# Batch 0's first attention with both token halves side by side in PSUM, strip-wise score passes for the last batch, and new instruction orders on five queues

## What is computed

```python
x = layernorm(x + attn(x))        # A: ternary-weight linear layers; softmax over the 16 heads of a token,
                                  #    plus a recurrent state over chunks of 128 tokens
x = layernorm(x + xattn(x, ctx))  # B: 32 query heads, 8 key heads, window 64, two sources (ctx and x)
x = layernorm(x + ffn(x))         # C: base linear layer + LoRA experts, top 2 of 8
```

## Time and profile before

| | us |
|---|---|
| median of 3 runs | 920.82 (917.58 to 921.01) |
| the profiled execution | 920.37 |
| its span, first to last instruction | 918.2 |
| PE busy | 805.0 (88%) |
| DVE busy | 515.8 (56%) |
| ACT busy | 322.8 (35%) |

### The profile page before, as it was taken

One profiled execution on the slowest core, in us unless ns is written; L12 is line 12 of the kernel. 1 busy time (PEld: TensorE's weight loads), 2 busy tenths in 40 slices (PEclk: granted clock), 3 DMA queues, 4 the chain that ended last, 5 costly groups with the idle time before them and its releaser, 6 DMA issues.

```text
span 918.2 us, 22670 instructions
## 1 busy us (share of the span) xinstructions
PE 805.0 (88%) x10223; PEld 518.4 (56%) x10275; DVE 515.8 (56%) x1061; ACT 322.8 (35%) x423; POOL 85.5 (9%) x103
## 2 busy tenths in 40 slices
PE   3888977888999989988899989988898978998996
PEld 2464763467635874467635864567545864474343
DVE  4645386437945487437845486447845383425233
ACT  5252323442243323442244323432244314230422
POOL 1102002000210012000300012000300010010001
PEclk9999999999999999999999999999999999999999
DMA  9512501000001000010001000010001000000000
GB/s 343 181 47 46 72 1 24 25 2 1 11 15 47 2 2 24 1 48 1 25 1 47 2 2 24 1 47 2 1 1 47 3 1 1 24 2 1 1 24 24
DMA packets 18879, 27.08 MB, mean 29 GB/s; under 512 B 5464, under 2 KB 7640, under 8 KB 18784
## 3 DMA queue, kind: packets, MB, share of 16 engines
q1 hardware_dynamic: 18640, 25.61, 9.3%
q10 hardware_dynamic: 144, 0.03, 0.0%
HBM read 21.44 MB, written 4.19 MB: 28 GB/s over the span
## 4 chain that ended last, share of the span: by engine, by line
PE 62%; DVE 19%; ACT 13%; issue 4%; POOL 1%; DMA 1%; ACTq 0%; POOLq 0%; SPq 0%; DVEq 0%
ACT p_b L740 9%; DVE max_b L1457 7%; PE ps L1118 7%; PE ps L1154 6%; PE ps L1039 6%; PE ps L1195 5%; PE ps L1022 4%; PE ps L1083 4%; PE ps L1059 3%; PE ps L870 2%; PE ps L943 2%; PE ps L1127 2%; PE ps L953 2%; PE ps L1047 2%; PE ps L838 2%
## 5 line engine op out<-in xcount | busy, mean ns | idle before, releaser
L740 ACT ACTIVATE p_b<-ps 128x2048 f32<-128x2048 f32 x64 | 106.5, 1664 | 116.1 <-PE ps L1127 116.1
L1457 DVE TENSOR_REDUCE max_b<-ps 128x4 f32<-128x768 f32 (+2 forms) x160 | 106.5, 709 | 39.5 <-PE ps L1097 21.3
L1083 PE MATMUL ps<-k_b,q_b 32*128 32x192 f32 (+2 forms) x1024 | 55.7, 332 | 25.7 <-DVE max_b L1457 23.6
L1118 PE MATMUL ps<-q_b,k_b 32*128 32x512 f32 (+1 forms) x512 | 66.2, 586 | 12.8 <-ACT p_b L740 7.0
L1483 DVE STREAM_TRANSPOSE o_nat<-ps 128x512 f32<-128x512 f32 x32 | 21.0, 695 | 98.2 <-PE ps L1143 98.2
L1083 PEld LDWEIGHTS ps<-k_b,q_b 32*128 32x128 f32 x1024 | 39.2, 184 | 43.1 <-DVE max_b L1457 37.1
L1143 PE MATMUL ps<-p_b,v_b 128*32 128x256 f32 (+1 forms) x1024 | 61.7, 358 | 2.0 <-ACT p_b L740 2.0
L1022 PE MATMUL ps<-c_t,wq 128*128 128x256 f32 x256 | 60.4, 385 | 2.9 <-DVE out_a L1380 1.9
L1337 DVE SCALAR_TENSOR_TENSOR nat<-ps,st_a,qkv_bias 128x512 f32<-128x512 f32 x48 | 35.3, 738 | 48.0 <-PE ps L870 47.7
L1195 PE MATMUL ps<-base_t,x_t 128*128 128x512 f32 x128 | 62.0, 609 | 0.3 <-DVE x L1562 0.3
L1039 PE MATMUL ps<-x_t,wq 128*128 128x256 f32 x256 | 60.0, 384 | 0.2 <-ACT x_t L694 0.2
(11 more groups left out here) (193 smaller groups left out, 1414.2 us busy)
## 6 DMA issues: line engine op xcount, KB each, us to landing
x_in<-x SPq DMA_DIRECT2D x8, 512.0 KB, 3.6
p_b<-ctx SPq DMA_DIRECT2D x8, 512.0 KB, 4.3
y<-x SPq DMA_DIRECT2D x7, 512.0 KB, 3.0
p_b<-L_attn_qkv_w SPq DMA_DIRECT2D x2, 1024.0 KB, 6.6
p_b<-L_xattn_Wq SPq DMA_DIRECT2D x1, 2048.0 KB, 14.8
x<-L_attn_qkv_w SPq DMA_DIRECT2D x2, 512.0 KB, 9.6
x<-L_ffn_base_w SPq DMA_DIRECT2D x2, 512.0 KB, 7.8
wo<-L_xattn_Wo SPq DMA_DIRECT2D x8, 128.0 KB, 7.5
```

What stands on the lines that cost most here:

```text
L740: act.activation(p_b[:, j % 2, :, 0:cols], ps[:, 4:8, 0:cols], ACT.Exp, scale=DB ** -0.5).then_inc(pb_here.sem, 1)
L1083: pe.matmul(bank(4 + r)[:, (i % 2) * N:(i % 2) * N + 2 * n * S], q_b[strip[r], i, :, :].rearrange("p h q -> p (h q)"), k_b[strip[r], half, ...
L1118: pe.matmul(bank(4 + r)[:, 0:nb * P], k_b[strip[r], half, 2 * j:2 * j + 2, :, :].rearrange("p c s k -> p (c s k)"), q_b[strip[r], 2 * j:2 ...
L1457: ins = dve.tensor_reduce(max_b[:, half, 0, i:i + k, 2 * n:2 * n + 2], ps[:, 4 + 2 * n:6 + 2 * n, :].rearrange("p r (i n) -> p i r n", i=2 ...
```

## The change

1. For batch 0 alone, half 1 of A uses banks 4 to 7 (`a_bank`), its own `maxp_0`, `maxt_0` and a `p_0` that lies over `q_b` and `k_b` (made one tile, `qk_b`). The order is `a2_s 0, a2_s 1, a2_m 0, a2_x 0, a2_m 1, a2_x 1, a2_v 0, a2_v 1` on PE; `a2_max 0, a2_max 1, a2_out 0, a2_out 1` on DVE; `b1_mix, a2_m 0, a2_m 1, a2_x 0, a2_x 1` on ACT. One more small load fills `maxp_0`.
2. `keep_on` goes out of `a2_m` (11), `a2_v` (6) and, for t = 1, `a2_s` (8).
3. The copy of the projection signs moves from DVE to ACT (`proj_keep`), between `a1_q` and `a1_v`; the two sums of absolute values move ahead, between two transposes of half 1. `proj_total` and `proj_scale` move behind `a2_rec`.
4. `base_turn 0` moves behind batch 1's `a1`, `base_turn 1` behind batch 1's six `a1_qkv`; ACT copies them ahead of batch 0's `a4`.
5. SP issues `mix` right after `late`, ahead of batch 0's context.
6. For batch 7, `b2` runs in two passes, strips 0 and 1 and then 2 and 3, and each waits only for the reduction of its own two banks; its `keep_on` goes out.
7. The lists of PE, DVE, ACT, POOL and SP are new. On PE the loop begins elsewhere in the same cycle, and inside it `b1_k` and `b1_q 0` go ahead of `a2_v 0`, `b1_v` behind it, `b2(0, 0)` ahead of `a2_x 1`, `a2_v 1` directly ahead of `a2_rec`; of C, `c2(1, 1)` goes ahead of `b3_s 3`. For batch 7, the parts of batch 6's `c2` are placed elsewhere among `b2` and `b3`.

```diff
+        def apart(b, t):
+            return isinstance(b, int) and b == 0 and t == 1
+        def a_bank(b, t):
+            return 4 if apart(b, t) else 0
...
             def a2_s(b, t, quarters):
-                    keep_on(b, 0, 8 if t else 4)
+                    keep_on(b, 0, 0 if t else 4)
...
+                        elif apart(b, t):
+                            pe.wait_ge(kept.sem, 3)
+                            pe.wait_ge(pkept.sem, 1)
                         else:
                             outa_here(pe, b, 1)
...
             def a2_m(b, t):
-                    keep_on(b, 0, 11)
...
             def a2_v(b, t):
-                    keep_on(b, 0, 6)
                     pa_here(pe, b, t + 1)
+                    src = p_0 if apart(b, t) else p_a
...
             def a2_x(b, t):
-                if t == 1:
+                if t == 1 and not apart(b, t):
                     oa_full(act, b, 1)
...
             def base_turn(b, part):
...
+                    out1(pe, 0)
+                    ct_here(pe, 0)
...
             def b2(b, half, pair):
-                keep_on(b, NB - 1, (0, 0, 6, 6, 4, 4, 2, 2)[4 * half + pair])
...
+                for strips in ((range(2), range(2, 4)) if alone else (range(4),)):
+                    if alone and pair:
+                        sb_max(pe, b, 8 * half + 2 * pair - 1 + strips[0] // 2)
...
```

The loop's order on PE around the second half of A, before and after:

```diff
-(B, of(b1_q, 1, range(2))), (A, of(a2_m, 1)), (B, of(b1_q, 1, range(2, KT))), (A, of(b1_c, 0)), (A, of(b1_c, 1)),
-(A, of(a2_x, 1, range(HT))), (B, of(b2, 0, 0)), (B, of(b2, 0, 1)), (A, of(a2_v, 1)), (B, of(b2, 0, 2)), (A, a2_rec),
+(B, of(b1_q, 1, range(2))), (A, of(b1_c, 0)), (B, of(b1_q, 1, range(2, KT))), (A, of(b1_c, 1)), (A, of(a2_m, 1)),
+(B, of(b2, 0, 0)), (A, of(a2_x, 1, range(HT))), (B, of(b2, 0, 1)), (A, of(a2_v, 1)), (A, a2_rec), (B, of(b2, 0, 2)),
```

More of the change, by code:

```diff
@@ L215, in program @@
         maxt_a = sb("maxt_a", [P, P], BF16)
+        maxp_0 = sb("maxp_0", [P, HT, S], BF16)
+        piece_0 = [maxp_0[:, :, p:3 * HT:3] for p in range(3)]
+        maxt_0 = sb("maxt_0", [P, P], BF16)
         sum_a = sb("sum_a", [P, HA, DA])
@@ L511, in c2 @@
                 sp.dma_start(one(ov, b), z_c[:, :, :]).then_inc(y_sent.sem, 16)
-            first = [(0, late), (0, b1), (1, a0), (2, a0), (1, mix)]
-            last = [(6, b1), (7, b1), (4, c2), (5, c2), (6, c2), (7, c2)]
-            run(sp, first, [(B, b1), (NEXT, a0), (D_, c2)], last)
+            first = [(0, late), (1, mix), (0, b1), (1, a0), (2, a0), (1, b1)]
+            last = [(7, b1), (4, c2), (5, c2), (6, c2), (7, c2)]
+            run(sp, first, [(D_, c2), (A, b1), (NEXT, a0)], last)
             y_sent(sp, NB - 1, 32)
@@ L916, in a2_s @@
                             rows = slice(a * S, (a + 1) * S)
-                            pe.matmul(bank(a), tokhot[rows, :], other[rows, :], start=True, stop=False)
+                            pe.matmul(bank(a_bank(b, t) + a), tokhot[rows, :], other[rows, :], start=True, stop=False)
                     for c in quarters:
@@ L1066, in b2 @@
             def b2(b, half, pair):
[L1067 to L1077 removed]
+                alone = isinstance(b, int) and b == NB - 1
@@ L1078, in b2 @@
+                if pair == 0:
+                    if half:
+                        mb_here(pe, b, 1)
+                    else:
+                        q_here(pe, b)
+                        k_here(pe, b)
+                        v_here(pe, b)
+                        if not alone:
+                            ct_here(pe, b + 1)
+                elif not alone:
+                    sb_max(pe, b, 8 * half + 2 * pair)
                 seen = [(i, slice(max(i - 2, 0), i + 1)) for i in (2 * pair, 2 * pair + 1)]
@@ L1079, in b2 @@
                 o = lambda r, i, n: bank(4 + r)[:, (i % 2) * N:(i % 2) * N + 2 * n * S].rearrange("p (c k) -> p c k", c=n)
-                for i, keys in seen:
-                    n = min(i, 2) + 1
-                    for r in range(4):
-                        pe.matmul(bank(4 + r)[:, (i % 2) * N:(i % 2) * N + 2 * n * S], q_b[strip[r], i, :, :].rearrange("p h q -> p (h q)"),
-                                  k_b[strip[r], half, keys, :, :].rearrange("p c s k -> p (c s k)"),
-                                  start=(i % 2 == 0), stop=False, skip_group_check=True)
@@ L1204, in _ @@
             first = [(-1, early), (0, a1), (0, of(a1_qkv, 0, [0])), (0, of(a1_qkv, 0, [1])), (0, of(a1_qkv, 0, [2])), (0, of(a1_qkv, 1, [0])),
-                     (0, of(a1_qkv, 1, [1])), (0, of(a1_qkv, 1, [2])), (0, a1_qt), (0, a1_state), (0, late), (0, of(a1_v, 0)), (0, of(a1_v, 1)),
-                     (0, of(a2_s, 0, range(HT))), (0, of(a2_m, 0)), (0, of(a2_x, 0, range(HT))), (0, proj_total), (0, of(a2_v, 0)),
-                     (0, of(a2_s, 1, range(HT))), (0, of(base_turn, 0)), (0, of(a2_m, 1)), (0, of(a2_x, 1, range(HT))), (0, of(base_turn, 1)),
@@ new lines, in _ @@
+                     (0, of(a1_qkv, 1, [1])), (0, of(a1_qkv, 1, [2])), (0, a1_state), (0, a1_qt), (0, late), (0, of(a1_v, 0)), (0, of(a1_v, 1)),
+                     (0, of(a2_s, 0, range(HT))), (0, of(a2_s, 1, range(HT))), (0, of(a2_m, 0)), (0, of(a2_x, 0, range(HT))), (0, of(a2_m, 1)),
+                     (0, of(a2_x, 1, range(HT))), (0, of(a2_v, 0)), (0, of(a2_v, 1)), (0, of(b1_c, 0)), (0, of(b1_c, 1)), (0, a2_rec), (0, proj_total),
+                     (0, of(b1_qc, 0, range(2))), (0, of(b1_qc, 0, range(2, KT))), (0, b1_kc), (0, a3_t), (0, of(a3, 0)), (0, of(a3, 1)), (1, a1),
@@ new lines, in _ @@
+                     (0, of(base_turn, 0)), (1, of(a1_qkv, 0, [0])), (1, of(a1_qkv, 0, [1])), (1, of(a1_qkv, 0, [2])), (1, of(a1_qkv, 1, [0])),
+                     (1, of(a1_qkv, 1, [1])), (1, of(a1_qkv, 1, [2])), (0, of(base_turn, 1)), (0, of(b1_qc, 1, range(2))), (1, a1_qt),
+                     (0, of(b1_qc, 1, range(2, KT))), (0, of(b1_x1, 0)), (0, of(b1_x1, 1)), (1, a1_state), (1, of(a1_v, 0)), (0, of(b1_v, range(2))),
+                     (1, of(a1_v, 1)), (0, of(b1_q, 1, range(2))), (1, of(a2_s, 0, range(HT))), (0, of(b1_q, 0, range(2))),
@@ L1354, in a2_max @@
                             dve.wait_ge(w_in.sem, W_IN)
+                    at = a_bank(b, t)
+                    part = piece_0 if apart(b, t) else piece
                     for n in range(2):
```

350 lines of the change are left out of this document (176 added, 174 removed).

## The result

The changed kernel takes 913.40 us (median of 14 runs, 911.25 to 916.12), the kernel before 918.51 on the same chip (14 runs, 915.84 to 921.21). The ratio is 0.9939, with a 95% interval of 0.9923 to 0.9955. That is faster by 5.1 us, against a forecast of 13.3. The profiled executions differ more, 920.37 against 913.30 us (spans 918.2 and 911.2). The profiled one of before lies in the upper part of its runs, so the traces show a gain of 7.0 where the medians show 5.1. The granted clock says why in part. The profiled one had 0.995. So what follows is read against an execution of before with more low clock than most of its executions have.

A forecast was written before the change was run, and what follows sets the result against it. It took PE as busiest (88%), with both ends bound by latency. Head -8.0, loop 0 and tail -5.3 summed to -13.3 us: 907.1 from the profiled 920.37, forecast 907, range 900 to 914.5.

The forecast's parts named there:

- the ladder: Batch 0's A block: with its two halves overlapped, the recurrent part is complete 10.8 us earlier, before the clock's cost.
- the 1.1 us that I took for `a2_x`: Batch 0's A block: one clock drop to 1.2 GHz, on `a2_x`, makes it 1.1 us late.
- the base weight: `base_turn` moved to batch 1's projections, with the reordered list there: +1.4 us up to batch 1's scores.
- the second part of the turn: `base_turn 1`, behind batch 1's `a1_qkv`: stands in full on the path, +1.1 us; the reordered list adds 0.8.
- The head: Start of the kernel up to the loop: -9.4 to the projection and +1.4 for the base weight, -8.0 us.
- the loop: Five rounds of 102.36 us: +0.2 us per round, set at 0, with -3 to +3 in all.
- batch 7's scores: Score stage of the last batch: split passes let DVE reduce without waiting, 6.3 us less.
- a rival at 0.14: Clock stays low without filler matmuls, in 43 to 50 and batch 7's passes: 911.5 us, chance 0.14.
- the tail: Batch 7's scores and the steps behind them: -6.3 and +1.0, -5.3 us, ends -8 and -3.
- The `c2` pieces among the exponentials: `c2(1, 1)` and `c2_lora 1` among batch 7's `b3` steps: 1.0 us lost.
- the split does little: Batch 7's scores: hand-over costs as much twice as once, tail 0 to -1, 912 us; chance 0.07.

The follow-up runs named there:

- g2: f4 with batch 0's two token halves one after the other again on PE, DVE and ACT: 922.31 us, ratio 1.0038 to the kernel before.
- f4: The changed kernel with batch 7's passes whole, filler matmuls back, and closing orders of PE, ACT and DVE as before: 909.92 us, ratio 0.9905 to the kernel before.
- f1: The changed kernel with five filler matmuls where PE waits 0.98 us for `k_b` ahead of batch 7's first score pass: 913.24 us, ratio 0.9941.
- f3: The kernel before with batch 7's score passes split and their filler matmuls kept: 921.07 us, ratio 1.0038.
- e4: The kernel before with only batch 7's score passes split, without filler matmuls: 926.97 us, ratio 1.0113.
- e1: The changed kernel with filler matmuls put back ahead of batch 7's score passes, split kept: 913.29 us, ratio 0.9942 to the kernel before.
- f2: f1 with batch 6's two closing `c2` pieces moved one place earlier each: 913.96 us, ratio 0.9949 to the kernel before.
- g4: f4 without filler matmuls ahead of any of batch 7's score passes: 911.96 us, ratio 0.9917 to the kernel before.

## Why the prediction was wrong

**Right: the ladder.** The halves overlap as rebuilt, the sum came at 58.98 for a forecast of 57.8, and g2, without the overlap, loses all of the gain. The clock's fall cost more than the 1.1 us that I took for `a2_x`: one low stretch of 6.83 us from 46.05 holds `a2_x 1` and nearly all of `a2_v 0`. The second exponential started 1.2 us after the first had ended, and DVE's first transpose came at 53.39 where I had 51.0 without the clock; 0.5 of that is a later start, and the other 1.9 go with the low clock.

**Wrong in sign, and in my favour: the base weight.** I had +1.4 us. From the recurrent sum to batch 1's scores the shift grew from 8.5 to 9.5 instead, so -1.0. No clock fell behind the turn, and `a1_qkv` gained 1.9 and not 1.0. From its end to batch 1's scores it takes 13.0 us instead of 12.6, +0.4, where I had added 1.9 for the second part of the turn and the new order. The head is -10 in the traces against -8.0 forecast. In medians f4 gives -8.1, which fits the profiled execution of before having more low clock than most.

**Right in the sum: the loop.** 102.42 for 102.36. Its parts were not taken one by one.

**Wrong: batch 7's scores, -6.3 in the forecast.** The step that failed is "A pass is half of about 1.2 us, less than half a reduction (0.91), so DVE goes through without a wait." Half a pass takes PE 0.98 us and not 0.6, since only the strips' running beside each other had made the whole one 1.22. Three things follow.
- A split round is 2.25 us at best, not 1.85 (f1, and half 1 after). Over six rounds that is 2.4 us.
- PE, no longer DVE, sets the pace: of 2.25 us it works 1.97, DVE 1.82. The pieces of `c2` and lora, which I priced at 0.6 and 0.7 us or left inside the turn, stand on the path in full, and so does any filler. f3 shows it with the clock at 2.4 GHz: a stage 2.3 us longer and a time 3.1 us longer than before, where I had -6.3.
- Without the filler PE fell to 1.2 GHz. I had this as a rival at 0.14, with 1.5 us for the tail "because DVE and ACT set the pace". Two rounds at 3.23 instead of 2.25 and one piece at 3.78 instead of 1.98 already are 3.8 us. e4 shows the full price, 6.7 us in one half. Filler would not have saved the gain, though: e1, with the filler and 3.41 us of low clock, takes as long (913.29) as the changed kernel (913.40).

The stage of 28.70 us is 8.1 over the 20.6 of the forecast. An estimate from the rows above: the low clock stands for 2.0 in half 0 (two rounds) and 1.8 in the turn (the piece of `c2`), which leaves some 4.3 for passes and pieces, 2.0 in half 0, 1.3 in the turn and 1.1 in half 1. So without the low clock the forecast would still have been far off.

The `c2` pieces among the exponentials cost 1.1, for 1.0 forecast. So the tail is +3.0 in the traces (+3.5 between f4 and the changed kernel) instead of -5.3, 8.3 off. The traces miss the forecast by 6.3 (7.0 for 13.3), since the head's surplus of 2.0 gave a part back. That the time lies within the range is luck: its upper end was the low clock plus a loss of 3 us in the loop, and the loop lost nothing. The rival that named the right place, "the split does little", had 0.07. Its reason, a hand-over cost paid twice, was not the right one either: the hand-over is 0.28 of the 2.25 us.

What stays open: which small differences decide where the clock falls. In this stage it first fell at 817.46 (after), 819.40 (f1), 824.68 (f2), 821.77 (g4) and not at all (f4).

## What to carry to other kernels

Before a pass is split so that its consumer can start earlier, look at how its matmuls run beside each other: if twice as many instructions take the same time (0.93 us for 16, 0.92 for 8), a split on that axis buys the overlap with producer time. Then ask which engine bounds the stage once the wait is gone, and price every other piece in that engine's queue again, since what was hidden before now counts in full. When a change bundles parts at two ends of a kernel, measure each end alone: here one end brought 8.1 us, and the other took 3.5 of it, most of that (2.8) by where other pieces had been put and not by the split.

## What the runs showed of the hardware that I had not expected

- Score matmuls on two of four 32-row strips run at half the rate of those on four: 0.92 us for eight against 0.93 for sixteen. The same pass takes 1.97 us instead of 1.22.
- The changed kernel's granted clock fell to half at 817.46 although PE was busy 3.53 of the 4 us from 814 to 818, with no gap over 0.98 us. Most of what it did there was 32-row score matmuls. With the same passes whole, wide `c2` pieces early and filler among them (f4) it stayed up in this stage although PE was busy for only 3.36 of the 4 us in 820 to 824. What makes the difference is not shown. The Trainium skill, page "TensorE: Matmul & The Clock Gate", says in its table "Why this matters for your kernels" that gaps in which PE is idle between bursts of matmuls bring the low clock back. Here it fell with no gap over 0.98 us between PE's rows, so the trace doesn't agree that gaps alone decide.
- The runs of one kernel lie in steps some 2 us apart. The changed kernel's 911.3 and 913.4 have the same mean clock, 0.986, and 915.2 to 916.1 go with 0.984 and 0.985. In the kernel before, the upper step goes with the clock (0.995 for 918.6 to 921.1), the lower two don't. What makes the steps was not found. It is why a single profiled execution can be off from the median by as much as half of the gain measured here.
